# Softmax sums of both query tiles in 128 columns, with one group joined on GpSimd, and a new beginning for a gated attention and FFN block

## The reference

```python
x = x + tanh(g_xattn) * xattn(layernorm(x), ctx)      # x: 16 x 256 x 512, ctx: 16 x 256 x 128
x = x + tanh(g_ffn) * ffn(layernorm(x))

def xattn(q, latent):                                  # 16 heads of 32
    qp = q @ Wq.T
    k, v = split(latent @ Wkv.T)
    scores = where(causal, qh @ kh.T / sqrt(32), lowest)
    return (softmax(scores) @ vh) @ Wout.T
def ffn(x):                                            # quantized to fp8 by rows, 512 -> 1408 -> 512
    qx = fp8(x / its row maximum);  g, u = qx @ fp8(Wg).T, qx @ fp8(Wu).T
    t = silu(g) * u
    return fp8(t / its row maximum) @ fp8(Wd).T
```

## Time and profile before

| | us |
|---|---|
| median of 3 runs | 734.01 (732.45 to 735.41) |
| the profiled execution | 735.42 |
| its span, first to last instruction | 733.7 |
| TensorE busy | 664.5 (91%) |
| VectorE busy | 664.1 (91%) |
| ScalarE busy | 549.0 (75%) |
| GpSimd busy | 546.5 (74%) |

### The profile page before, as it was taken

One profiled execution on the slowest core, in us unless ns is written; L12 is line 12 of the kernel. 1 busy time (PEld: TensorE's weight loads), 2 busy tenths in 40 slices (PEclk: granted clock), 3 DMA queues, 4 the chain that ended last, 5 costly groups with the idle time before them and its releaser, 6 DMA issues.

```text
span 733.7 us, 15607 instructions
## 1 busy us (share of the span) xinstructions
PE 664.5 (91%) x6130; PEld 417.8 (57%) x6130; DVE 664.1 (91%) x1099; ACT 549.0 (75%) x987; POOL 546.5 (74%) x606
## 2 busy tenths in 40 slices
PE   1567889999999999999999999999999999999774
PEld 1456566656666666656565756566666666545331
DVE  5987687999898989999999989999999999899993
ACT  6888768788878796978878787879687868565540
POOL 5777878986868787887878787969597777766551
PEclk9889799999999999999999999999999999999896
DMA  8979875888685749666775757876667664613313
GB/s 308 227 144 201 165 135 99 160 147 158 102 158 92 166 79 195 93 150 110 139 121 136 131 116 143 123 150 112 143 104 147 94 143 76 126 37 78 74 29 96
DMA packets 151207, 95.51 MB, mean 130 GB/s; under 512 B 115326, under 2 KB 121854, under 8 KB 151134
## 3 DMA queue, kind: packets, MB, share of 16 engines
q1 hardware_dynamic: 148974, 92.68, 64.9%
q0 software_dynamic: 576, 1.45, 0.7%
q10 hardware_dynamic: 1584, 0.39, 0.3%
HBM read 31.59 MB, written 9.83 MB: 56 GB/s over the span
## 4 chain that ended last, share of the span: by engine, by line
PE 50%; DVE 24%; ACT 9%; POOL 6%; DMA 5%; issue 2%; SPq 2%; ACTq 0%; POOLq 0%; DVEq 0%
PE pair L1163 30%; PE pair L1401 3%; PE pair L1406 3%; DVE room L2889 3%; PE pair L1432 2%; DVE tm L3240 2%; PE pair L1433 2%; DVE room L3235 2%; POOL PT L799 2%; PE pair L1428 2%; DVE room L2885 2%; DVE mx L3052 2%; DVE room L3278 2%; DVE room L3191 2%; PE pair L1384 1%
## 5 line engine op out<-in xcount | busy, mean ns | idle before, releaser
L835 POOL TENSOR_TENSOR room<-room,up_scale 128x512 f32<-128x512 f32 (+1 forms) x96 | 128.3, 1348 | 38.6 <-ACT room L2303 38.4
L3052 DVE TENSOR_REDUCE mx<-pair 128x6 f32<-128x768 f32 x128 | 116.7, 950 | 4.3 <-PE pair L1339 4.1
L799 POOL TENSOR_SCALAR_AFFINE_SELECT PT<-PT 128x512 f32<-128x512 f32 x128 | 105.6, 854 | 12.4 <-ACT PT L2221 11.7
L2221 ACT ACTIVATE PT<-pair 128x768 f32<-128x768 f32 x128 | 98.0, 816 | 19.3 <-PE pair L1384 16.3
L2303 ACT ACTIVATE room<-room,sx 128x512 f32<-128x512 f32 (+1 forms) x96 | 63.9, 679 | 43.3 <-DVE sx L3156 26.2
L1163 PE MATMUL pair<-WgT,room 128*128 128x512 bf16 (+1 forms) x384 | 91.1, 367 | 4.6 <-DVE room L3235 4.5
L1163 PE MATMUL pair<-WdT,room 128*128 128x512 bf16 x352 | 83.5, 387 | 11.6 <-DMA room<-room 11.6
L1163 PE MATMUL pair<-xT,WqTh 128*128 128x256 bf16 x512 | 88.5, 276 | 4.0 <-ACT x L1979 4.0
L1163 PE MATMUL pair<-WuT,room 128*128 128x512 bf16 (+1 forms) x384 | 91.6, 364 | 0.1
L1163 PE MATMUL pair<-xT,WqTl 128*128 128x256 bf16 x256 | 70.5, 276 | 0.0
L3235 DVE TENSOR_TENSOR room<-pair,room 128x512 f32<-128x512 f32 (+1 forms) x96 | 60.7, 636 | 9.8 <-POOL x L844 6.5
(11 more groups left out here) (137 smaller groups left out, 1854.4 us busy)
## 6 DMA issues: line engine op xcount, KB each, us to landing
xin<-in_x_dram SPq DMA_DIRECT2D x16, 512.0 KB, 4.8
x<-in_x_dram SPq DMA_DIRECT2D x16, 512.0 KB, 3.9
K<-kh SPq DMA_DIRECT2D x32, 256.0 KB, 5.7
Q<-qh SPq DMA_DIRECT2D x32, 256.0 KB, 4.9
out_dram<-x SPq DMA_DIRECT2D x16, 512.0 KB, 3.2
K<-kl SPq DMA_DIRECT2D x16, 256.0 KB, 6.8
Q<-kl SPq DMA_DIRECT2D x16, 256.0 KB, 4.9
room<-in_L_ffn_w_down_dram SPq DMA_DIRECT2D x4, 704.0 KB, 8.0
```

What stands on the lines that cost most here:

```text
L799: pool.affine_select(out=view, in_=view, compare_op=ALU.is_ge, fill=0.0, base=0, pattern=[[0, 2], [0, 2], [1, P]], channel_multiplier=-1). ...
L835: pool.tensor_tensor(g, g, up_scale[:, chunk(n)[1]], ALU.mult).then_inc(slw_done, 1)
L2221: act.activation(head_columns(ring(b, c), 0, 384), head_columns(shifted_pair[c][:, :], 0, 384), ACT.Exp, scale=SCALE).then_inc(exp_done, 1)
L3052: dve.tensor_reduce(mx[:, heads, :], head_columns(w, 0, 3 * P).rearrange("p h (r s) -> p h r s", s=P), AX.X, ALU.max).then_inc(max_done, 1)
```

## The change

1. **Sums in 128 columns.** `pick` has eight variants of 32 columns: query tile t of group g goes to rows KT * t + g of its 32, so both query tiles' sums stand in the same 128 columns. Each group now runs three sets of four matmuls of 128 columns in place of a set of 256 and one of 128 columns. `sums_inverted` takes 128 columns, not 256, and `inverse_spread` makes eight shuffles of 128 columns a block, not four of 256.
2. **One group joined.** For group 0 (`JOINED = (0,)`) GpSimd adds key tile 1's probabilities of query tile 1 to key tile 0's (`joined`, 128 x 512, into R), so this group has two sets of matmuls, not three. `joined` stands behind `causal_part(b, 1)` in GpSimd's list, ahead of `added`, and `weighted(b, 0)` waits for it.
3. **Beginning.** SP loads Wkv, then x(0), ahead of the w_down units. The constant rows are put into Q4 and K4 by four VectorE copies (29 partitions x 4096 bf16, `put_queries`, `put_keys`), not by SP's DMAs. VectorE rounds units 0 to 4, 6, 8, 10, 12, 14, GpSimd the other six. The turns of Wq and of Wkv's keys permute in TensorE's identity matrix (`by_place`), so that the copies behind them are contiguous.
4. **Orders.** All five lists are written anew (waits and PSUM banks with them), in the beginning, in the loop and at the end. In the loop `up_products(k + 1, 5)` now stands ahead of `weighted(k + 3, 0)`, and on VectorE `up(k - 1, 3)` stands directly behind `down_scaled(k - 2, 1)`, where `largest_x` stood between.

```diff
-        pick = sb("pick", [P, KT, HD])
+        pick_flat = sb("pick_flat", [P, TT * KT * (HD + 1)])
-        rsum = sb("rsum", [P, S])
+        rsum = sb("rsum", [P, P])
+        def joined_keys(g):
+            return R[:, g % 2 * 2:g % 2 * 2 + 2, :].rearrange("p a (h s) -> p (a h) s", h=2)
...
             load_w_kv()
+            load_x(0)
+            unit_loaded(2)
             unit_loaded(3)
-            unit_loaded(2)
+            load_c(0)
+            unit_loaded(0)
             unit_loaded(1)
-            unit_loaded(0)
-            load_x(0)
-            load_c(0)
             load_w_q()
+            turn_x(0, 0)
+            load_x(1)
+            turn_x(0, 1)
             load_w_out()
-            mask_of_queries(0)
...
             stack_keys(0, 1)
+            unit_loaded(7)
+            unit_loaded(6)
             stack_keys(0, 2)
...
             unit_loaded(8)
             stack_queries(0, 0)
             stack_queries(0, 1)
             stack_queries(0, 2)
...
+            def joined(b, g):
+                pool.wait_ge(cut_done, 8 * b + 2)
+                first = (NC * b + 2 * g) % RING
+                heads = PT[:, first:first + 2, :].rearrange("p c n -> p (c n)").rearrange("p (h n) -> p h n", h=G)
+                pool.tensor_tensor(joined_keys(g), heads[:, :, 0:P], heads[:, :, 2 * P:3 * P], ALU.add).then_inc(join_done, 1)
...
             def weighted(b, g):
-                pe.wait_ge(cut_done, 8 * b + 2 * g + 2)
                 if g == 0:
+                    pe.wait_ge(join_done, b + 1)
...
-                for t in range(TT):
+                for j in range(G):
+                    pe.matmul(sum_bank[HD * j:HD * j + HD, 0:P], pick[:, g, :], probabilities(b, 2 * g + j // 2, j % 2, 0)[:, 0:P],
+                              start=(g == 0), stop=False, skip_group_check=True)
+                if g in JOINED:
                     for j in range(G):
-                        last = pe.matmul(sum_bank[HD * j:HD * j + HD, t * P:S], pick[:, g, :],
-                                         probabilities(b, 2 * g + j // 2, j % 2, t), start=(g == 0 and t == 0),
-                                         stop=(g == KT - 1 and t == TT - 1), skip_group_check=True)
+                        last = pe.matmul(sum_bank[HD * j:HD * j + HD, 0:P], pick[:, KT + g, :], joined_keys(g)[:, j, :],
+                                         start=False, stop=(g == KT - 1), skip_group_check=True)
+                else:
+                    for j in range(G):
+                        pe.matmul(sum_bank[HD * j:HD * j + HD, 0:P], pick[:, KT + g, :], probabilities(b, 2 * g + j // 2, j % 2, 0)[:, P:S],
+                                  start=False, stop=False, skip_group_check=True)
+                    for j in range(G):
+                        last = pe.matmul(sum_bank[HD * j:HD * j + HD, 0:P], pick[:, KT + g, :], probabilities(b, 2 * g + j // 2, j % 2, 1),
+                                         start=False, stop=(g == KT - 1), skip_group_check=True)
...
+            def put_queries(i):
+                if i == 0:
+                    dve.wait_ge(const, N_CONST)
+                dve.tensor_copy(Q4[i][96:MASK_END, :, :].rearrange("r h (t s) -> r (h t) s", t=TT),
+                                rows_q[96:MASK_END, None, :].to_broadcast([MASK_END - 96, NH * TT, P])).then_inc(q_put, 1)
...
             def sums_inverted(b):
                 dve.wait_ge(group_made, 4 * b + 4)
-                dve.reciprocal(rsum[:, :], sum_bank[:, 0:S]).then_inc(rsum_done, 1)
+                dve.reciprocal(rsum[:, :], sum_bank[:, 0:P]).then_inc(rsum_done, 1)
...
-                dve.stream_shuffle(out=R[:, 2 * h, :], in_=rsum[:, :], mask=[2 * h] * HD)
-                dve.stream_shuffle(out=R[:, 2 * h + 1, :], in_=rsum[:, :], mask=[2 * h + 1] * HD).then_inc(r_spread, 1)
+                for g in range(2 * h, 2 * h + 2):
+                    for t in range(TT):
+                        last = dve.stream_shuffle(out=R[:, g, tok(t)], in_=rsum[:, :], mask=[KT * t + g] * HD)
+                last.then_inc(r_spread, 1)
```

More of the change, by code:

```diff
@@ new lines, in _ @@
+            turn_qt(8, 1)
+            stack_queries(12, 0)
+            stack_queries(12, 1)
+            stack_queries(12, 2)
+            turn_qt(9, 0)
+            store(8)
+            turn_qx(10, 0)
+            load_c(14)
+            load_x1(11)
+            turn_x(13, 0)
+            turn_x(13, 1)
+            load_x(14)
+            no_maxima(13)
+            turn_qx(10, 1)
+            stack_keys(13, 0)
+            stack_keys(13, 1)
+            stack_keys(13, 2)
+            turn_qt(9, 1)
@@ new lines, in _ @@
+            stack_queries(13, 0)
+            stack_queries(13, 1)
+            stack_queries(13, 2)
+            store(9)
+            load_c(15)
+            turn_qt(10, 0)
+            turn_qx(11, 0)
+            turn_x(14, 0)
+            turn_x(14, 1)
+            load_x(15)
+            no_maxima(14)
+            load_x1(12)
+            stack_keys(14, 0)
+            turn_qx(11, 1)
+            turn_qt(10, 1)
+            stack_keys(14, 1)
+            stack_keys(14, 2)
+            stack_queries(14, 0)
@@ new lines, in _ @@
+            normalised_low(2, 0)
+            normalised_low(2, 1)
+            keys_low(4, 0)
+            keys_low(4, 1)
+            up_scaled(1, 0)
+            added(0, 0)
+            max_parts(3)
+            up_scaled(1, 1)
+            up_scaled(1, 2)
+            scales1(5)
+            up_scaled(1, 3)
+            up_scaled(1, 4)
+            queries_low(4, 0)
+            causal_part(3, 0)
+            causal_part(3, 1)
+            joined(3, 0)
+            added(0, 1)
+            causal_part(3, 2)
@@ L1608, in _ @@
             shifted(1, 4)
+            unit_turned(12)
             values(2, 0)
             shifted(1, 5)
+            weighted(1, 0)
             shifted(1, 6)
-            weighted(1, 0)
+            values(2, 1)
             shifted(1, 7)
             weighted(1, 1)
-            unit_turned(13)
+            scores(2, 0)
             weighted(1, 2)
             weighted(1, 3)
-            values(2, 1)
+            spread(6)
+            unit_turned(15)
             unit_turned(14)
-            gate_products(0, 0)
-            up_products(0, 0)
-            scores(2, 0)
+            unit_turned(13)
             scores(2, 1)
+            keys(3, 0)
+            keys(3, 1)
             scores(2, 2)
@@ L1852, in _ @@
             weighted(13, 3)
+            values(14, 0)
+            down(11, 0)
+            values(14, 1)
+            up_products(12, 0)
             scores(14, 0)
[L1854 to L1856 removed]
+            scores(14, 1)
             gate_products(12, 0)
[L1858 to L1859 removed]
             scores(14, 2)
@@ new lines, in _ @@
+            maxima(2, 0)
+            rounded_x(0, 0)
+            sums_inverted(1)
+            inverse_spread(1, 0)
+            normalised(1, 0)
+            inverse_spread(1, 1)
+            normalised(1, 1)
+            floored_x(0, 1)
+            maxima(2, 1)
+            lifted_x(0, 1)
+            maxima(2, 2)
+            rounded_x(0, 1)
+            maxima(2, 3)
+            gate(0, 0)
+            residual(1, 0)
+            maxima(2, 4)
+            scale_x(0)
+            maxima(2, 5)
@@ L3470, in _ @@
[L3470 to L3488 removed]
+                rounded_x(k, 0)
```

3037 lines of the change are left out of this document (1510 added, 1527 removed).

## The result

The change makes the kernel 2.0% slower: median 748.51 us (746.22 to 749.67, 4 runs) against 733.66 beside it, ratio 1.0198 with a 95% interval of 1.0169 to 1.0227. The span of the profiled execution grows from 733.7 to 747.6 us. The forecast was 726.5, its range 718 to 737.

The account below looks back on a forecast made before the run. TensorE was taken to bound the middle (477.94 of 480 us busy), VectorE close behind. From 735.42, −5 (beginning), −2.5 (sums) and −0.5 (tail) gave 727.4, scaled to the runs' median 726.0, stated as 726.5; range 718 to 737.

Parts of the forecast that it names:

- The sums on TensorE and VectorE: Sums in 128 columns: TensorE gains 0.21 us a block, 2.5 in all, in the joined group; VectorE −0.5 a block.
- The beginning: Start up to block 2: block 0's scores 11 us earlier, its maxima 7.5; 5 us kept at block 2's turned maxima.
- B: Rival for the start: the beginning gains nothing because VectorE is the bound there; 731 us, chance 0.20.
- C: Rival for the start: put copies take 5.3 us each and the beginning loses some 8.5 us; 739.5 us, chance 0.08.
- The join: GpSimd's addition in each block, 1.27 us: hidden by GpSimd's spare 8.2 us, VectorE's longer wait fitting its room; priced at 0.
- room: VectorE's idle time in a middle block, 1.8 us, with 0.5 won by the sums: 2.3 together to take up the wait.
- the 2.5 us that the join was to win on TensorE: Middle blocks: the joined group has two sets, 0.44 us for 0.65; 0.21 a block over 12.4 blocks, taken as 2.5.
- Rival D: Middle blocks: the join stretches VectorE by 1.3 us and up(., 3) waits 1.9 longer, +11 us; 739.5 us, chance 0.10.
- its point of decision (2.3 us): Rival D in the middle blocks: it decides from 2.3 us of VectorE loss a block on, 1.9 already spent.
- the tail: The end of the kernel, where VectorE is on the path: one block's worth of cheaper sums, −0.5 us.

Follow-up runs that it names:

- no_join: The change without the join, group 0 having three sets of matmuls like the others: 737.63 us, ratio 1.0035 to the kernel before.
- lists_only: The change's beginning and lists with the sums of before (256 and 128 columns, four shuffles) and no join: 740.07 us, ratio 1.0078.
- sums_only: The kernel before with its own lists and beginning, only the sums in 128 columns added, no join: 735.55 us, ratio 1.0009.
- dve_load: The kernel before plus two useless VectorE maxima over 128 x 512 in each of the loop's eight passes: 742.49 us, ratio 1.0100.
- join_last: The kernel before with its own lists, sums in 128 columns and the join for group 3 behind causal_part(b, 7): 751.50 us, ratio 1.0216.
- change_join_last: The change with the join for group 3 behind causal_part(b, 7), TensorE waiting only ahead of the set reading it: 749.07 us, ratio 1.0184.
- change_y_store: The change, join kept, with down_scaled's second tile in its own buffer and SP's store behind turn_qt and stack_queries in the loop: 744.61 us, ratio 1.0130.
- the last pair: Kernel before's lists, 128-column sums, down_scaled's second tile in its own buffer, added and SP's lines moved: with the join in added's place 772.24 us, without join 765.89.
- no_join_y: The change without the join, with down_scaled's second tile in a buffer of its own: 737.29 us, ratio 1.0023.

## Why the prediction was wrong

Where the time went is read from the turned maxima of blocks 4 and 12 and the end (us from the start):

| | block 4 | block 12 | end | block 12 to end |
|---|---|---|---|---|
| before | 223.7 | 535.0 | 733.7 | 198.7 |
| the change | 221.4 | 541.6 | 747.6 | 206.0 |
| no_join | 216.5 | 530.5 | 736.4 | 205.9 |
| lists_only | 217.7 | 532.1 | 737.9 | 205.8 |

Without the join the beginning's lead is 7.2 us at block 4; up to block 12 the lists lose 2.7 of it, and behind block 12 another 7.2. The join costs 541.6 − 530.5 = 11.1 up to block 12 and 0.1 behind it. −7.2 + 2.7 + 11.1 + 7.3 = +13.9, the difference of the spans. So in the last blocks of the new lists, which are longer already without it, the join is free.

- **The sums on TensorE and VectorE: right in price.** 0.66 for 0.65, a reciprocal of 0.95 for 0.96, a shuffle's pitch of 0.21. sums_only shows no change of the time, and VectorE is busy for 36.06 us a block there, not 36.53: the forecast −0.5.
- **The beginning: right up to block 2.** Scores at 55 for 53, maxima at 57.5 for 57, a put copy 1.22 for 1.3. At block 2 no_join leads by 145.4 − 139.8 = 5.6, where I took 5; in the change, with two joins ahead of this point, 3.5 of it is gone. Rivals B and C are out.
- **The join: the step that failed.** "It just fits. I price it at 0" set VectorE's idle time (1.8 us) and its new gain (0.5) as room against a wait of 1.9. The wait came out so: 2.53 − 0.73 = 1.8, of which 0.73 comes with the new lists (no_join waits 1.46) and 1.07 with the join. The room did not: dve_load measures 0.15 us of it. In the change VectorE's idle time is (241.58 − 217.94) / 6 = 3.94 us a block for 2.17, so it grew by the whole of the wait and took up none of it, and the period grew by 1.56. Nor did the 2.5 us that the join was to win on TensorE come, since TensorE is no longer full (233.37 of 241.58). That the rest of VectorE's idle time is waits of the same round, which do not shrink when it gets later, fits this and is not shown wait by wait.
- **Rival D, which had 0.10, is nearest:** VectorE's wait for `added` sets in as it says. But its price rested on a stretched VectorE as well, and its point of decision (2.3 us) on the same room. In the change VectorE's instructions are not stretched: it is busy for 217.94 / 6 = 36.3 us a block, in no_join for 36.2, and the line of the earlier trace rows takes 0.743 us in the mean from block 4 to block 10, for 0.926 before. The stretch came in join_last.
- **The lists: a term that is missing.** I named them in the change and gave the new loop and the new end no price. lists_only has the loop's blocks at 39.39, 0.7 over before, and the end 7.1 us longer, where the sum had 0.5 less for the tail.

What is shown is that the join makes 11.2 of the 13.9 us by which the span grew, that it costs 0.78 us a block in the loop of the change and 1.15 to 1.34 in the lists of before, and who waits in each run: SP's queue, `up(., 3)`, TensorE's groups, or VectorE by stretched instructions. Its price is not fixed. It is 0.25 to 0.32 us a block in change_join_last, in change_y_store and between the last pair, and next to nothing behind block 12 of the change. That the whole stretch of GpSimd from the first exponentials to the last causal part is on the round with no slack is argued from these; the run that was to show it did not.

Two losses stay open. Why the first blocks of change_join_last lose 7.4 us was not tried. Nor was what in the new lists loses 7 us behind block 12. Of these, 119.7 − 115.1 = 4.6 lie between the turned maxima of blocks 12 and 15 (no_join and before), the rest behind them. no_join_y is no faster than no_join beyond what the runs can tell, but there the wait of `up(., 3)` was replaced by that of `up(., 5)`, so a late `up(., n)` is not excluded.

## What to carry to other kernels

In a loop whose engines hand work round in order, an engine's idle time need not be room: add a known amount of useless work to it and see how much the period grows, before you place an operation there. When one chain of waits is shown, look for others of the same length before you take its cause for the cause; here several took each other's place. And rewritten orders need a term of their own in the sum, their tail above all.

## What the runs showed of the hardware

In four blocks of join_last a VectorE instruction ended only behind the GpSimd instruction that had started ahead of it: the `tensor_scalar` that starts 0.27 us behind the join's start ends 0.15 us behind its end, 1.16 us long for 0.34. From 260 to 460 us `tensor_scalar` on 128 x 512 bf16 takes 0.858 us in the mean of ten, in sums_only 0.532; the subtraction of the same size 0.940 for 0.422. The Trainium skill, page "SBUF — State Buffer", section "Who interferes with whom", says that `tensor_scalar` can enter the modes in which VectorE contends with GpSimd and that the one that comes second is fully blocked; the row at 327.52 agrees.
